# Four layers of attention on 64-node graphs: weighted sums on 64x64 tiles, output biases added by GpSimd, fewer row-term products

## What is computed

```python
h = jnp.maximum(_layernorm(x, axis=-1), 0.0)
x = x + layer(h, adj, ...)
```

```python
q, k, v = split_heads(x @ Wq + bq), split_heads(x @ Wk + bk), split_heads(x @ Wv + bv)   # biases in layer 0 only
attn = jax.nn.softmax(jnp.where(mask, einsum('bhid,bhjd->bhij', q, k) * scale, neg), axis=-1)
out = einsum('bhij,bhjd->bhid', attn, v)
return out @ Wo + bo
```

```python
Wh = jnp.einsum('bni,hoi->bhno', h, W) + bW[None, :, None, :]
e = jnp.einsum('bhno,hop->bhnp', Wh, attn)
A_mat = jnp.tanh(jnp.where(adj, jnp.einsum('bhnp,bhmp->bhnm', e, Wh), 0.0))
hp = jax.nn.relu(jnp.einsum('bhnm,bhmo->bhno', A_mat, Wh))
ha = concat(hp) @ A_w.T;  hf = h @ fc_w.T
coeff = jax.nn.sigmoid(hf @ g1_w.T + ha @ g2_w.T + gbias)
return hf * coeff + ha * (1.0 - coeff)
```

## Time and profile before

| | |
|---|---|
| runs | 2065.01, 2065.45, 2073.82 us |
| profiled execution, span | 2068.7 us |
| PE busy | 1916.0 us (93%) |
| DVE busy | 1272.5 us (62%) |
| ACT busy | 957.6 us (46%) |
| POOL busy | 157.4 us (8%) |
| mean granted clock of PE | 0.978 |

### The profile page before, as it was taken

The page is one execution under the profiler, slowest core; times in us unless marked ns, Lnnn a source line. Parts: engine busy times, 40 slices in busy tenths (PEclk is TensorE's granted clock), DMA queues, the critical chain, the costliest instruction groups (busy, mean ns, idle before and its releaser), DMA issues.

```text
span 2068.7 us, 53790 instructions
## 1 busy us (share of the span) xinstructions
PE 1916.0 (93%) x21934; PEld 1720.2 (83%) x21934; DVE 1272.5 (62%) x3513; ACT 957.6 (46%) x3544; POOL 157.4 (8%) x169
## 2 busy tenths in 40 slices
PE   7599999999999999999999999999999999999997
PEld 6488888888888888888888888888888888888886
DVE  3466666666666666566666666666666666656663
ACT  3344544544554544454554454454454454454452
POOL 0000000000000000000000000000000000000000
PEclk8699999999999999999999999999999999999998
DMA  6000000000000000000000000000000000000000
GB/s 190 1 3 13 13 12 13 7 8 13 13 12 11 13 2 13 13 12 12 12 3 12 13 13 11 13 3 12 13 12 11 13 3 12 13 13 11 12 7 6
DMA packets 36517, 30.45 MB, mean 15 GB/s; under 512 B 11568, under 2 KB 36144, under 8 KB 36336
## 3 DMA queue, kind: packets, MB, share of 16 engines
q1 hardware_dynamic: 36336, 27.55, 4.5%
HBM read 19.15 MB, written 8.39 MB: 13 GB/s over the span
## 4 chain that ended last, share of the span: by engine, by line
PE 86%; DVE 5%; ACT 5%; issue 3%; DMA 1%; POOL 0%; SPq 0%; POOLq 0%; DVEq 0%; ACTq 0%
PE ps L445 79%; PE ps L518 4%; PE ps L594 3%; ACT probs L792 3%; DVE probs L1006 1%; DVE small L918 1%; DVE x L1015 1%; ACT oT L802 1%; ACT hT L767 1%; PE ps L714 1%; DMA raw_mats<-mats 1%; DVE small L1004 0%; DMA x<-x 0%; POOL small L422 0%; DVE xn L936 0%
## 5 line engine op out<-in xcount | busy, mean ns | idle before, releaser
L445 PE MATMUL ps<-hT,w_hi 128*128 128x256 f32 x2560 | 500.2, 289 | 11.9 <-ACT hT L767 11.7
L445 PEld LDWEIGHTS ps<-hT,w_hi 128*128 128x128 f32 x2560 | 412.6, 192 | 29.5 <-ACT hT L767 24.1
L445 PE MATMUL ps<-w_hi,hT 128*128 128x256 f32 (+1 forms) x1536 | 430.2, 344 | 0.0
L792 ACT ACTIVATE probs<-probs,small 128x64 f32<-128x64 f32 x1024 | 341.4, 335 | 102.4 <-DVE small L996 101.8
L445 PE MATMUL ps<-hT,w_lo 128*128 128x256 f32 x1280 | 338.9, 285 | 0.0
L445 PEld LDWEIGHTS ps<-w_hi,hT 128*128 128x128 f32 x1536 | 272.5, 189 | 39.9 <-issue 6.5
L445 PE MATMUL ps<-w_lo,hT 128*128 128x256 f32 (+1 forms) x768 | 250.9, 338 | 0.0
L445 PEld LDWEIGHTS ps<-hT,w_lo 128*128 128x128 f32 x1280 | 245.6, 192 | 0.7
L422 POOL TENSOR_TENSOR small<-small,consts 128x2 f32<-128x2 f32 x128 | 94.1, 736 | 1669.2 <-DVE small L928 1669.1
L445 PE MATMUL ps<-w_hi,oT 128*128 128x256 f32 x768 | 183.5, 305 | 28.0 <-DVE oT L857 28.0
L792 ACT ACTIVATION_READ_ACCUMULATOR probs<-probs,small 128x1 f32 x1024 | 192.5, 188 | 0.0
(11 more groups left out here) (105 smaller groups left out, 3377.2 us busy)
## 6 DMA issues: line engine op xcount, KB each, us to landing
raw_mats<-mats SPq DMA_DIRECT2D x8, 1024.0 KB, 11.9
x<-x SPq DMA_DIRECT2D x32, 256.0 KB, 2.8
out<-xn SPq DMA_DIRECT2D x32, 256.0 KB, 2.9
adj<-adjq SPq DMA_DIRECT2D x64, 16.0 KB, 2.0
adjT<-adjt SPq DMA_DIRECT2D x64, 8.0 KB, 1.8
raw_consts<-board_consts SPq DMA_DIRECT2D x1, 515.5 KB, 3.6
w_bias<-rows SPq DMA_DIRECT2D x1, 256.0 KB, 5.3
bias_cols<-cols SPq DMA_DIRECT2D x1, 6.0 KB, 3.9
```

The lines of the kernel that those rows point to most:

```text
L445: return nc.tensor.matmul(o, lhsT, rhs, start=start, stop=stop, skip_group_check=True)
L792: last = fn(p, p, ACT.Exp, bias=ROWMAX[s][:, row:row + 1], accum_out=ROWSUM[s][:, row:row + 1])
```

## The change

- `av` is cut into products of 64x64: for each column block the two graphs e and the two halves f of the features, in the order (0,0), (1,1), (0,1), (1,0). The operands are the same; there are 32 products a step in place of 16.
- No row-picking product stands at the end of `tokens_out` any more, so that `v` of layer 0 has 12 products in place of 14 and each `out` 6 in place of 7. The output biases of the three attention layers are spread over 128 partitions once, in the preparation (`BOB`); the value bias goes into the one of layer 0, multiplied with Wo, since the weights of a softmax sum to one. In each attention layer POOL adds `BOB` to x, 128x512, as soon as `xn` has been computed, and DVE's addition in `out` waits for that (`x_bias`).
- Row terms: `UVEC` holds the rounded part and the rest in different columns (100 in place of 36), so that `r` is four products; the two graphs of a tile have their rows in different partitions, so that `row_terms` is 128x512 and `s2` needs two products. ACT and DVE split the rows in two instructions each in place of one.
- `ORDER` is new for all four engines (lags 45, 41, 44, 36 become 40, 43, 44, 45). On PE the list of what follows what is nearly the same. Of slot 1's work beside slot 0's layer 0, one `wh` now stands between slot 0's two `pt` steps, both `av` steps stand before `heads`, and one `ha` before `out`, so that less lies between slot 0's last `out` and its next `turn`. Beside slot 1's layer 0, slot 0's steps stand as they did. On DVE the `pv` and `out` of layer 1 come one step earlier, and some `wh` additions stand among the masks.
- In the preparation there are two more products for the value bias, seven instructions for the output biases, two copies of them by ACT and some small copies by DVE; POOL starts its passes after the copies by ACT.

```diff
 LO = 32
-RH = LO + H2
...
-            at = C_RT + P * half + SQ * half
-            c[rows, at:at + SQ] = 1
+    for e in range(2):
+        for part in (SQ * e, SQ * e + H2, SQ * e + LO):
+            rows = np.arange(part, part + H2)
+            c[rows, C_HEADS + rows - part] = 1
+            c[rows, C_RT + SQ * e:C_RT + SQ * e + SQ] = 1
     c[:, C_HALF] = -0.5
...
@@ -421,21 +427,27 @@
                     pool.wait_ge(sm["ve"], n)
                     nc.gpsimd.tensor_tensor(RSTD[s], VE[s], HALF.broadcast_to([P, TT]), ALU.pow
                                             ).then_inc(sm["rstd"], 1)
+                elif k == "norm" and a != L2:
+
+                    pool.wait_ge(sm["xn_ready"], norm_halves(a, v)[1])
+                    x = X[s][:, :].rearrange("p (t d) -> p t d", t=TT)
+                    nc.gpsimd.tensor_tensor(x, x, BOB[:, a:a + 1, :].broadcast_to([P, TT, D]), ALU.add
+                                            ).then_inc(sm["x_bias"], 1)
                 elif k == "r":
 
                     pool.wait_ge(sm["r_lo"], v.once)
                     nc.gpsimd.tensor_tensor(
-                        R4[s][:, :].rearrange("p (b h q) -> p b h q", h=H2, q=SQ),
-                        RS[s][:, :].bitcast(F32).rearrange("p (b q) -> p b q", q=SQ).unsqueeze(2).broadcast_to([P, NB, H2, SQ]),
-                        HEADS.unsqueeze(1).unsqueeze(3).broadcast_to([P, NB, H2, SQ]), ALU.mult
+                        R4[s][:, :, :, :], RS[s][:, :, :].bitcast(F32).unsqueeze(2).broadcast_to([P, TT, H2, SQ]),
+                        HEADS.unsqueeze(1).unsqueeze(3).broadcast_to([P, TT, H2, SQ]), ALU.mult
                         ).then_inc(sm["r4_ready"], 1)
...
             last.then_inc(setup["terms_zero"], 1)
+            pool.wait_ge(setup["bo_sb"], 1)
             passes(pool, step, ORDER["pool"])
...
@@ -459,8 +471,12 @@
             pe.wait_ge(setup["consts"], 2)
             pe.wait_ge(setup["rows"], 4)
             for n in range(2):
-                last = mm(PS[:, 6 + n, :], SELR[:, 0, :], ROWS[:, n * 512:n * 512 + 512], True, True)
+                last = mm(PS[:, 6 + n, :], SELR[:, 0, :], RAWROWS[:, n * 512:n * 512 + 512], True, True)
             last.then_inc(setup["bw_ps"], 1)
+
+            for c in range(DC):
+                last = mm(PS[:, 5, c * P:c * P + P], RAWROWS[:, c * P:c * P + P], SELR[:, 1, :], True, True)
+            last.then_inc(setup["bv_ps"], 1)
...
+            for n in range(3):
+                o = PS[:, 5 + n // 2, n % 2 * D:n % 2 * D + D]
+                last = mm(o, SELR[:, 1, :], RAWROWS[:, (n + 1) * D:(n + 1) * D + D], True, n > 0)
+                if n == 0:
+                    pe.wait_ge(raw_sems[0], 48)
+                    for c in range(DC):
+                        mm(o, BVB[:, c, :], RAWM[:, 3, c, :], False, c == DC - 1)
+            last.then_inc(setup["bo_ps"], 1)
...
@@ -546,9 +572,7 @@
                 for c in range(DC):
                     if ready and t == 0:
                         pe.wait_ge(ready[1], halves[c])
-                    last = mm(o, actT(1, c)[:, at], WHI[:, m, c, :], False, bias is None and c == DC - 1)
-                if bias is not None:
-                    last = mm(o, SELR[:, 1, :], ROWS[:, bias * D:bias * D + D], False, True)
+                    last = mm(o, actT(1, c)[:, at], WHI[:, m, c, :], False, c == DC - 1)
                 return last
...
             def l2(s, k, i, v):
                 sm, n = S[s], v.once
@@ -623,14 +647,11 @@
                     transposed_h(s, L2, i, v)
                 elif k == "r":
 
-                    o = bank(s, 1)[0:RH, 0:TOK]
-                    for c in range(DC):
-                        pe.wait_ge(sm["hT_hi"], norm_halves(L2, v)[c])
-                        mm(o, UVEC[:, 0, c, :], HT[s][:, 0, c, :], c == 0, False)
-                        mm(o, UVEC[:, 1, c, :], HT[s][:, 0, c, :], False, False)
-                    for c in range(DC):
-                        pe.wait_ge(sm["hT_lo"], norm_halves(L2, v)[c])
-                        last = mm(o, UVEC[:, 0, c, :], HT[s][:, 1, c, :], False, c == DC - 1)
+                    o = bank(s, 1)[0:RW, 0:TOK]
+                    for j, ready in enumerate((sm["hT_hi"], sm["hT_lo"])):
+                        for c in range(DC):
+                            pe.wait_ge(ready, norm_halves(L2, v)[c])
+                            last = mm(o, UVEC[:, c, :], HT[s][:, j, c, :], j == 0 and c == 0, j == 1 and c == DC - 1)
                     last.then_inc(sm["r_ps"], 1)
...
@@ -659,10 +680,9 @@
                         pe.wait_ge(sm["e_dve"], v.two[1])
                         pe.wait_ge(sm["r4_ready"], n)
                         alone(pe)
-                        for b in range(NB):
-                            t, e = divmod(b, 2)
-                            mm(bank(s, S2_BANKS[t])[:, 0:TOK], SELR[:, 3 + e, :], R4[s][:, b * TOK:b * TOK + TOK],
-                               e == 0, False)
+                        for t in range(TT):
+                            mm(bank(s, S2_BANKS[t])[:, 0:TOK], SELR[:, 3, :],
+                               R4[s][:, t, :, :].rearrange("p h q -> p (h q)"), True, False)
...
@@ -678,9 +698,9 @@
                     alone(pe)
                     for m in range(H2 * DC):
                         h = m // DC
-                        for e in range(2):
-                            last = mm(bank(s, AV_BANKS[i][e])[:, m * SQ:m * SQ + SQ],
-                                      WH[s][SQ * e:SQ * e + SQ, i, m * P:m * P + P],
+                        for e, f in ((0, 0), (1, 1), (0, 1), (1, 0)):
+                            last = mm(bank(s, AV_BANKS[i][e])[SQ * f:SQ * f + SQ, m * SQ:m * SQ + SQ],
+                                      WH[s][SQ * e:SQ * e + SQ, i, m * P + SQ * f:m * P + SQ * f + SQ],
                                       A[s][SQ * e:SQ * e + SQ, i, h * SQ:h * SQ + SQ], True, True)
                     last.then_inc(sm["av_ps"], 1)
...
             split_hi(4, len(SPLITS))
+            act.wait_ge(setup["bo_ps"], 1)
+            fn(BOB[:, 0:2, :], PS[:, 5, :], ACT.Copy)
+            last = fn(BOB[:, 2, :], PS[:, 6, 0:D], ACT.Copy)
+            last.then_inc(setup["bo_sb"], 1)
...
                     act.wait_ge(sm["r_ps"], n)
-                    fn(RS[s][0:RH, :], bank(s, 1)[0:RH, 0:TOK], ACT.Identity, bias=S0[:, :]
-                       ).then_inc(sm["r_hi"], 1)
+                    for e in range(2):
+                        own = slice(SQ * e, SQ * e + LO + H2)
+                        last = fn(RS[s][own, :, :], r_view(s, e)[own, :, :], ACT.Identity, bias=S0[own, :])
+                    last.then_inc(sm["r_hi"], 1)
...
@@ -1011,6 +1046,7 @@
                 elif k == "out":
 
                     at = slice(i * D, i * D + D)
+                    dve.wait_ge(sm["x_bias"], n)
                     dve.wait_ge(sm["y_ps"], v.six[2 * a + i])
                     tt((XN if a == 2 else X)[s][:, at], bank(s, Y_BANKS[i])[:, 0:D], X[s][:, at], ALU.add
                        ).then_inc(sm["res"], 1)
@@ -1028,8 +1064,11 @@
                 elif k == "r":
 
                     dve.wait_ge(sm["r_hi"], n)
-                    stt(RS[s][LO:RH, :], bank(s, 1)[LO:RH, 0:TOK], S0[LO:RH, :],
-                        RS[s][LO:RH, :].bitcast(F32), ALU.add, ALU.subtract).then_inc(sm["r_lo"], 1)
+                    for e in range(2):
+                        low = slice(SQ * e + LO, SQ * e + LO + H2)
+                        last = stt(RS[s][low, :, :], r_view(s, e)[low, :, :], S0[low, :],
+                                   RS[s][low, :, :].bitcast(F32), ALU.add, ALU.subtract)
+                    last.then_inc(sm["r_lo"], 1)
```

More of the change, by code:

```diff
@@ L43 @@
 MASKED = -1e30
-ATT = [dict(layer=0, heads=8, mats=0, bias=1), dict(layer=1, heads=4, mats=4, bias=2),
-       dict(layer=3, heads=4, mats=8, bias=3)]
+ATT = [dict(layer=0, heads=8, mats=0), dict(layer=1, heads=4, mats=4), dict(layer=3, heads=4, mats=8)]
 HEADS_AT = [((0, 4), (1, 5), (3, 2), (6, 7)), ((0, 1), (3, 2)), ((0, 1), (3, 2))]
@@ L84, in constants @@
     c[[1, 3, 5], C_SELAB + 1] = 1
-    for part in (0, LO):
-        rows = np.arange(part, part + H2)
-        c[rows, C_HEADS + rows - part] = 1
-        for half in range(2):
-            at = C_RT + P * half + SQ * half
-            c[rows, at:at + SQ] = 1
+    for e in range(2):
[3 more added lines that the diff above has]
+            c[rows, C_RT + SQ * e:C_RT + SQ * e + SQ] = 1
     c[:, C_HALF] = -0.5
@@ L167, in build @@
         CVEC = sb("c_vec", [P, DC, H2], F32)
-        UVEC = sb("u_vec", [P, 2, DC, RH], F32R)
-        S0 = sb("s0", [RH, 1], F32)
+        UVEC = sb("u_vec", [P, DC, RW], F32R)
+        S0 = sb("s0", [RW, 1], F32)
         IDENT = CF[:, 0:P]
@@ L502, in _ @@
             for c in range(DC):
[L503 removed]
+                last = mm(PS[0:RW, 4, 0:H2], BPAD[:, c, :], A1[:, c, :], c == 0, c == DC - 1)
             last.then_inc(setup["vec_ps"], 1)
@@ L534, in features_out, with tokens_out @@
```

(6 more changed lines are left out.)

66 lines of the change are left out of this document (40 added, 26 removed), and 32 rows, old and new, of the table ORDER.

## The result

The changed kernel takes 2100.85 us (median; 2092.19 to 2111.41) against 2067.38 us before it in the same job: a ratio of 1.0162, 95% interval 1.0125 to 1.02. It is slower by 33 us. Forecast were 1984 us with a range of 1961 to 2013, so forecast and range are both wrong, and the sign with them. The profiled execution took 2111.41 us and is the slowest of the four. In later jobs four single runs took far longer than their neighbours (2467.26, 2632.13, 4647.39 and 7448.76 us) and are left out of the medians.

What follows compares the result with a forecast made beforehand. PE, busy 93% of the span with products end to end, was taken as the bound. 2068.7 - 98.1 leaving PE + 14 given back + 2.5 preparation = 1987.1, less 3.3 for the median: 1984 us, range 1961 to 2013.

Steps and rivals of the forecast that it cites:

- What leaves PE: On PE: shorter weighted sums save 52 us, 256 bias products 30.7, 128 row terms 15.4; together 98 us.
- What POOL adds: POOL's 96 additions, 1.31 us each, 126 us in all, are covered before `out` wants them; costed at nothing.
- POOL gives way: Reading of one meeting: POOL's power took 1.06 instead of 0.70 us beside a DVE addition, which took its usual 0.68.
- The rival that carried it: Rival in which POOL's additions hold up DVE writing hT, up to 1.31 us each: 2110 us, chance 0.05.
- The moved step: POOL's queue: slot 1's `row_terms` goes behind slot 0's next power, with e, wh and more before `s2`.
- The clock: PE's granted clock: changed waits of layer 3 may make low stretches more or less frequent; 10 us either way.
- What is given back: PE's waits in layer 3 and both slots' layer 0 take back 0.9 us a turn, 14 us (0 to 26).
- (b): Slot 0's layer 0: row-product saving lost, second weighted sum waits for its `wh`; 0.5 us a turn (0 to 0.9).
- Preparation: Before the loop: the new bias chain delays POOL's first power by 2.5 us, once (1 to 5).
- Rivals 1 and 2: First: weighted sums save nothing, spacing 0.028, 2040 us, chance 0.04. Second: chains take back half, 2016 us, chance 0.13.

Runs made afterwards that it cites:

- PE's waits filled: Changed kernel plus 16 unread products of 256 columns a pass in PE's waits of layer 3: 2068.82 us, ratio 1.0.
- the additions without readers: Changed kernel with POOL's additions replaced by 504-element additions of constant tiles into an unread tile, nobody waiting, output biases missing: 2088.41 us, ratio 1.0116 to the kernel before.
- the kernel with the additions moved: Changed kernel with POOL's additions behind the scores (layer 1: q) and POOL's order laid out anew: 2029.45 us, ratio 0.9804 to the kernel before.

## Why the prediction was wrong

The gap of 117 us to the forecast divides by the medians of three kernels: 2100.85 to 2068.82, the same with PE's waits filled, is 32 us of clock; 2068.82 to 2007.91, the additions and POOL's order moved (two things at once), is 61 us of POOL, of which up to 16 are again the lower clock, behind the waits that POOL makes; 2007.91 to 1984 leaves 24. The filling products cost something themselves (512 x 0.12 = 61 us if none of them lay in a wait; but the waits for `probs` fell from 60.1 us to 14.3), so the clock's part is at least 32, if the filling does nothing but hold the clock up, and what is left of the forecast's own error at most 24.

**What leaves PE: right.** Step, form and count are as predicted. The kernel with the additions moved has 62 us less of PE's busy time in fourteen turns than the kernel before, at a lower mean clock.

**What POOL adds: the step that failed.** "I cost it at nothing": the sum asked who waits for POOL's result, and nobody does (the additions without readers cost nearly as much). It didn't ask whom POOL holds while it works. The row was there, and I read it as "POOL gives way". What it shows is that DVE had started first, at 1000.09, and POOL at 1000.26. It says nothing of who would give way in the other order, and an addition that starts when `xn` is half written is first by its place. The rival that carried it had the mechanism and the length (1.31 us for each against the 1.27 in the trace) and got 0.05. That its 2110 us lies near 2101 is luck: it has the additions alone, at full length each, and nothing for `row_terms`, for the clock or for the 24 us left. It had the place wrong as well: the operation that writes `hT` reads PSUM and isn't held; `xn` and the masks ahead of it are. Without the additions the changed kernel is 57 us faster, 0.60 us for each of 96; it isn't 1.31, for part of the holding lies where PE has other work.

**The moved step.** "`row_terms` of slot 1 now stands behind slot 0's next power but has e, wh and more before `s2`": again its reader, not its neighbour. Behind the power it starts in the moment in which DVE, released by the same power, writes `xn`. In the kernel before that shift, for both slots, costs 80 us, more than any other edit that was run apart. In the change the instruction is half as long; at the prediction's own 1.3 us (1.92 less 0.6), held 32 times, it would have been up to 42 us. That alone wouldn't have turned the sign.

**The clock: a term mis-sized.** Allowed were 10 us either way; at least 32 came, and at least 30 with the weighted sums alone. The mechanism was named ("what the waits of layer 3 become"), its size taken from a kernel in which PE hardly ever pauses. The forecast treated it as noise about the sum. But the kernel with nothing but shorter weighted sums has 165 us at the lower level for 91, and 28 low stretches in layer 3 for 8: it came with the saving itself, and so had one sign. Whether the shorter steps or the longer pauses beside them bring it wasn't separated.

**What is given back: not refuted.** 14 us were forecast (0 to 26). 24 us are left over in all, part of it the filling, so at most 38 were given back; how much of the 24 belongs here isn't shown. The wait for `probs` is 60.6 us against 58.6, over 70 places in place of 39. In slot 0's layer 3 the two pairs of transposes wait 0.42 and 1.09 us, where the second alone waited 1.45. (b) is seen at its size in the step above. PE's idle time for which the profile names no releaser ("issue") rose from 17.9 to 26.8 us, part of it in a weighted sum of slot 1; what it is stays open.

**Preparation: nearly right.** The first product of the loop starts 3.5 us later (58.9 against 55.42); 2.5 were forecast, 1 to 5 allowed.

**Rivals 1 and 2.** The spacing in the weighted sums is that of the forecast, and the chains don't take back half: with POOL out of the way and PE's waits filled, 59.5 us are gained on the kernel before, 24 short of the forecast's 83.

## What to carry to other kernels

Before work goes to GpSimd because it is idle, ask not only who waits for it but which instructions of VectorE would start while it runs, at every place where it lands, and lay it where VectorE reads from PSUM; the same for each instruction that moves behind another in GpSimd's queue. In a kernel like this one, with PE busy 93% of the time, a saving beside a wait can be worth less than its products, since the clock may follow (5 us of 42 to 52 here); a mean clock that falls between two profiles is a term of the sum. An engine's order is a part of the change with a price of its own: here, in the kernel before, that of the least busy engine cost 80 us, and those of the three others nothing.

## What the runs showed of the hardware

Whom POOL holds: a `tensor_scalar` from SBUF to SBUF (0.73 to 1.37, 1.67 and 2.23 us for two, beside instructions of 1.05, 1.27 and 1.91 us) and a bf16 `tensor_tensor` (0.43 to 1.39 us); not an operation with one input in PSUM (0.76 us). An instruction is held for the remaining time of the other less 0.15 to 0.27 us in these four meetings, so a collision costs by its length, and by who is first.

Work of no use made kernels faster: 480 to 512 unread products gave 21.5, 30 and 32 us, as the granted clock in the fourteen turns rose (0.96 to 0.99 in the changed kernel, 0.98 to 1.00 with the additions moved) and the stretches at the lower clock in layer 3 went (31 to 0 and 19 to 1).

Products of 64x64 that go in turn to the four quarters of the array start 0.017 us apart (1.09 us for 64), where those of 64x128 start 0.06 us apart (1.93 us for 32): twice the instructions take little more than half the time.
